# Norm statistics and residual moved from VectorE to ScalarE and TensorE in a recurrent block with routed experts

## The reference

```python
x = layernorm(x + attn(x))          # over the 256 channels, no gain
x = layernorm(x + experts(x))
```

```python
kv  = k_t[i] * v_t[j]
y_t = sum_i r_t[i] * (S[i, j] + u[i] * kv)
S   = w_t[i] * S + kv
```

## Time and profile before

| | |
|---|---|
| median of three runs | 2342.44 us |
| the profiled execution, its own time | 2343.03 us |
| its span, first to last instruction | 2341.3 us |
| mean granted TensorE clock | 0.922 of 2.4 GHz |
| PE (TensorE matmul) busy | 1938.1 us (83%) |
| DVE (VectorE) busy | 1834.2 us (78%) |
| POOL (GpSimd) busy | 1373.3 us (59%) |
| ACT (ScalarE) busy | 1059.1 us (45%) |
| 1400 to 2280 us, the experts: PE busy | 875.23 us |
| 2280 to 2342 us, the last norm: ACT, DVE busy | 37.65 us, 32.24 us |

### The profile page before, as it was taken

How to read it: one execution, slowest core, us unless ns; L and a number is a source line. 1 busy time by engine, 2 the same in 40 slices (tenths; PEclk the granted TensorE clock), 3 DMA queues, 4 the chain that set the end, 5 groups by cost and what they waited for, 6 DMA issues and landing times. The chain is left out here.

```text
span 2341.3 us, 33041 instructions
## 1 busy us (share of the span) xinstructions
PE 1938.1 (83%) x9894; PEld 1336.8 (57%) x9894; DVE 1834.2 (78%) x3157; ACT 1059.1 (45%) x1919; POOL 1373.3 (59%) x954
## 2 busy tenths in 40 slices
PE   5777888788777887877776299999999999999980
PEld 2333343333333333433332189999999999999970
DVE  2899999899999998999997266666666666666655
ACT  2233553345334543444432255555555555555546
POOL 3667787768777787678775224444444444454440
PEclk9889999899989998999886599999999999999995
DMA  6932111111112111111020144545454545455538
GB/s 163 220 87 64 46 46 54 47 54 36 51 47 58 29 51 42 58 29 49 31 69 20 58 122 121 122 121 120 120 120 122 120 120 121 120 123 122 124 57 287
DMA packets 172844, 209.00 MB, mean 89 GB/s; under 512 B 12796, under 2 KB 152480, under 8 KB 172768
## 3 DMA queue, kind: packets, MB, share of 16 engines
q1 hardware_dynamic: 112688, 143.09, 20.7%
q0 software_dynamic: 28672, 34.78, 8.6%
q10 hardware_dynamic: 31408, 30.33, 5.0%
HBM read 118.65 MB, written 75.53 MB: 83 GB/s over the span
## 5 line engine op out<-in xcount | busy, mean ns | idle before, releaser
L807 DVE TENSOR_TENSOR_SCAN S<-wT,S,vb 128x512 f32<-128x512 f32 x512 | 624.9, 1262 | 0.0
L1070 POOL TENSOR_TENSOR prod<-S,rT 128x2048 f32<-128x2048 f32 x128 | 536.8, 4198 | 148.0 <-DVE S L807 147.8
L1289 PE MATMUL up<-x_parts,w_parts 128*128 128x308 f32 x3072 | 464.2, 307 | 1.5 <-DVE x_parts L1402 1.5
L1304 PE MATMUL down<-w_parts,h_parts 128*128 128x512 f32 (+1 forms) x1280 | 452.4, 396 | 0.0
L1289 PEld LDWEIGHTS up<-x_parts,w_parts 128*128 128x128 f32 x3072 | 439.2, 189 | 4.1 <-issue 1.8
L1364 POOL TENSOR_TENSOR ye<-ye,weight 128x256 f32<-128x256 f32 (+1 forms) x160 | 197.7, 1235 | 379.9 <-DVE ye L1458 379.9
L1342 ACT ACTIVATE h_full<-up,b_now 128x616 f32<-128x616 f32 x256 | 198.6, 776 | 421.2 <-PE up L1289 409.6
L1372 POOL DMA_INDIRECT sums<-ye,sum_at x160 | 281.6, 1760 | 150.1 <-POOL ye L1364 140.0
L1445 DVE TENSOR_TENSOR h_parts<-h_full,h_parts 128x616 fp32r<-128x616 f32 x256 | 206.8, 808 | 193.1 <-ACT h_parts L1342 192.8
L1307 PE MATMUL down<-w_parts,h_parts 128*128 128x256 f32 (+1 forms) x1280 | 357.4, 279 | 0.0
L571 PE MATMUL vb<-v_stack,pick_v 128*128 128x512 f32 x512 | 216.7, 507 | 152.0 <-DVE S L807 151.8
(11 more groups left out here) (176 smaller groups left out, 2645.2 us busy)
## 6 DMA issues: line engine op xcount, KB each, us to landing
w_raw<-in_L_ffn_w_dram SPq DMA_DIRECT2D x64, 1024.0 KB, 8.8
expert_in_rows<-y_tok ACTq DMA_DIRECT2D x30, 652.5 KB, 9.1
xe<-expert_in_rows SPq DMA_DIRECT2D x32, 522.0 KB
v_stack<-v_parts SPq DMA_DIRECT2D x64, 256.0 KB, 4.5
x_tok<-in_L_attn_x_dram SPq DMA_DIRECT2D x16, 512.0 KB, 3.3
x_res<-in_L_attn_x_dram SPq DMA_DIRECT2D x16, 512.0 KB, 3.4
sums<-x_row SPq DMA_DIRECT2D x16, 512.0 KB, 2.9
rows<-sums SPq DMA_DIRECT2D x16, 512.0 KB, 5.5
```

The lines of the kernel that those rows point to most:

```text
L807: dve.tensor_tensor_scan(line[:, 1:TC + 1], wT[:, par, half, :], vb[:, p % 2, g, :], line[:, 0:1], ALU.mult, ALU.add).then_inc(scanned, 1)
L1070: pool.tensor_tensor(prod[:, q % 2], S[:, q % RING, :, 0:TC], rT[:, par, half, None, :].to_broadcast([P, QUAD, TC]), ALU.mult).then_inc(pr ...
L1289: last = pe.matmul(up[:, f % 2, half, 0:HC], w1_parts[:, par, wp, k, f * P:(f + 1) * P], x_parts[:, par, xp, k, half * HC:(half + 1) * HC] ...
L1304: pe.matmul(down[0:m, (par * TILES + t) % 2, :, :], h_parts[:, 0, f, t * P:t * P + m], w2_parts[:, par, :, f, :], start=f == 0, stop=False)
```

## The change

`stat1` and `stat2` leave VectorE. ScalarE drains y tile by tile with a sum along the 256 columns (`accum_out`), scales the sums to the negated mean, and takes the squares of the rows less the mean, again with a sum; the root then takes the sum of squares with a scale of 1/256. The residual leaves VectorE too: TensorE adds x_res by a matmul with the identity into the same accumulation as the projection, and ScalarE drains the result into x1, with sums. In `C_AT` the steps from "stat1" to "root2" come one slot sooner; "norm2", "x1T", "gate", "top" and "ratio" come one slot later; "count", "place" and "scatter" stay. In the last norm a partition holds four successive rows instead of rows that lie 128 apart.

```diff
@@ -186,8 +186,9 @@
         y_tok = sb("y_tok", [P, TPC, C])
         x_res = sb("x_res", [P, TPC, C])
         x1_row = sb("x1_row", [P, TPC, C + FIELDS])
-        stats = sb("stats", [P, 2, TPC, 6])
-        mv = sb("mv", [P, 2, TPC, 2])
+        total = sb("total", [P, 2, TPC])
+        square = sb("square", [P, 2, TPC])
+        squares = sb("squares", [P, TPC, C])
         rstd = sb("rstd", [P, 2, TPC])
         offset = sb("offset", [P, 2, TPC])
         minus_mean = sb("minus_mean", [P, 2, TPC])
@@ -259,6 +260,7 @@
         res_loaded = sem("res_loaded")
         x1_stored = sem("x1_stored")
         s_dve = sem("s_dve")
+        squared = sem("squared")
         root_done = sem("root_done")
         normed = sem("normed")
         tanh_done = sem("tanh_done")
@@ -320,13 +322,13 @@
         NSHORT = len(DVE_MIXES) * NH
         XM_OF = {"w": 0, "k": 1, "v": 2, "r": 0}
 
-        C_AT = {"turn": 6, "stat1": 9, "root1": 10, "norm1": 12, "back": 14, "wo0": 17, "z0": 18, "wo1": 19,
-                "z1": 20, "stat2": 21, "root2": 22, "norm2": 23, "x1T": 25, "gate": 27, "top": 28, "ratio": 28,
+        C_AT = {"turn": 6, "stat1": 8, "root1": 9, "norm1": 11, "back": 13, "wo0": 16, "z0": 17, "wo1": 18,
+                "z1": 19, "stat2": 20, "root2": 21, "norm2": 24, "x1T": 26, "gate": 28, "top": 29, "ratio": 29,
                 "count": 30, "place": 30, "scatter": 31}
         NCF = 10
 
-        LN1_AT = 2 * TPC + 1
-        X1_AT = LN1_AT + 2 * TPC + 1
+        LN1_AT = 1
+        X1_AT = LN1_AT + 1
         GAP_AT = X1_AT + 2 * TPC + 1
         HITS_AT = GAP_AT + 4
         NCH = HITS_AT + 2
@@ -527,11 +529,15 @@
                         last.then_inc(c_full, 1)
                     if s == C_AT[f"wo{k}"]:
                         c_fill(i, 4 + k)
+                        if k == 0:
+                            pe.wait_ge(res_loaded, stage_value(i, 16, 16))
                         for t in range(2):
+                            pe.matmul(pc[:, t * C:(t + 1) * C], ident[:], x_res[:, 2 * k + t, :],
+                                      start=True, stop=False)
                             for h in range(NH):
                                 at = (2 * k + t) * P
                                 last = pe.matmul(pc[:, t * C:(t + 1) * C], yT[:, h, at:at + P],
-                                                 wo_sb[:, h, :], start=h == 0, stop=h == NH - 1)
+                                                 wo_sb[:, h, :], start=False, stop=h == NH - 1)
                         last.then_inc(c_full, 1)
                     if s == C_AT["x1T"] + k:
                         c_fill(i, 6 + k)
@@ -716,37 +722,9 @@
                 dve.wait_ge(root_done, stage_value(i, 2, which + 1))
                 dve.reciprocal(rstd[:, which, :], rstd[:, which, :]).then_inc(s_dve, 1)
 
-            def statistics(src, which):
-                for t in range(TPC):
-                    dve.bn_stats(stats[:, which, t, :], src[:, t, :]).then_inc(s_dve, 1)
-
             def stage_c(i, par, s):
-                if s == C_AT["stat1"]:
-                    dve.wait_ge(c_drained, stage_value(i, NCF, 2))
-                    statistics(y_tok, 0)
-                    chain(i, TPC)
-                    dve.sem_inc(wait_carrier, 1)
-                    for t in range(TPC):
-                        dve.bn_aggr(mv[:, 0, t, :], stats[:, 0, t, :]).then_inc(s_dve, 1)
                 if s == C_AT["norm1"]:
                     invert(i, 0)
-                for k in range(2):
-                    if s == C_AT[f"z{k}"]:
-                        dve.wait_ge(c_full, stage_value(i, NCF, 5 + k))
-                        if k == 0:
-                            dve.wait_ge(res_loaded, stage_value(i, 16, 16))
-
-                            wait_from(dve, x1_stored, stage_value(i, 16, 0))
-                            wait_from(dve, scattered, stage_value(i, 16 * 2 * TPC, 0))
-                        dve.tensor_tensor(x1[:, 2 * k:2 * k + 2, :], pc[:].rearrange("p (t c) -> p t c", t=2),
-                                          x_res[:, 2 * k:2 * k + 2, :], ALU.add).then_inc(c_drained, 1)
-                if s == C_AT["stat2"]:
-                    dve.wait_ge(c_drained, stage_value(i, NCF, 6))
-                    statistics(x1, 1)
-                    chain(i, LN1_AT + TPC)
-                    dve.sem_inc(wait_carrier, 1)
-                    for t in range(TPC):
-                        dve.bn_aggr(mv[:, 1, t, :], stats[:, 1, t, :]).then_inc(s_dve, 1)
                 if s == C_AT["norm2"]:
                     invert(i, 1)
                 if s == C_AT["top"]:
@@ -907,8 +885,19 @@
                         if isinstance(i, int) and i == 0:
 
                             act.wait_ge(s_fill, 16 * FILLS)
-                        act.activation(y_tok[:, 2 * k:2 * k + 2, :], pc[:].rearrange("p (t c) -> p t c", t=2),
-                                       ACT.Copy).then_inc(c_drained, 1)
+                        for t in range(2):
+                            ins = act.activation(y_tok[:, 2 * k + t, :], pc[:, t * C:(t + 1) * C], ACT.Copy,
+                                                 accum_out=total[:, 0, 2 * k + t:2 * k + t + 1])
+                        ins.then_inc(c_drained, 1)
+                    if s == C_AT[f"z{k}"]:
+                        act.wait_ge(c_full, stage_value(i, NCF, 5 + k))
+                        if k == 0:
+                            wait_from(act, x1_stored, stage_value(i, 16, 0))
+                            wait_from(act, scattered, stage_value(i, 16 * 2 * TPC, 0))
+                        for t in range(2):
+                            ins = act.activation(x1[:, 2 * k + t, :], pc[:, t * C:(t + 1) * C], ACT.Copy,
+                                                 accum_out=total[:, 1, 2 * k + t:2 * k + t + 1])
+                        ins.then_inc(c_drained, 1)
                     if s == C_AT["back"] + k:
                         act.wait_ge(c_full, stage_value(i, NCF, 3 + k))
                         for h in range(NH):
@@ -919,13 +908,22 @@
                         act.wait_ge(c_full, stage_value(i, NCF, 7 + k))
                         act.activation(yT[:, :, 2 * k * P:(2 * k + 2) * P], pc[:].rearrange("p (h t) -> p h t", h=NH),
                                        ACT.Copy).then_inc(c_drained, 1)
+                for which, (name, rows) in enumerate((("stat1", y_tok), ("stat2", x1))):
+                    if s == C_AT[name]:
+                        act.wait_ge(c_drained, stage_value(i, NCF, 2 + 4 * which))
+                        act.activation(minus_mean[:, which, :], total[:, which, :], ACT.Copy, scale=-1.0 / C
+                                       ).then_inc(mean_kept, 1)
+                        act.wait_ge(mean_kept, stage_value(i, 2, which + 1))
+                        for t in range(TPC):
+                            ins = act.activation(squares[:, t, :], rows[:, t, :], ACT.Square,
+                                                 bias=minus_mean[:, which, t:t + 1],
+                                                 accum_out=square[:, which, t:t + 1])
+                        ins.then_inc(squared, 1)
                 for which, name in enumerate(("root1", "root2")):
                     if s == C_AT[name]:
-                        act.wait_ge(s_dve, stage_value(i, NCH, (2 * TPC, LN1_AT + 2 * TPC)[which]))
-                        act.activation(rstd[:, which, :], mv[:, which, :, 1], ACT.Sqrt, bias=eps_col[:, 0:1]
-                                       ).then_inc(root_done, 1)
-                        act.activation(minus_mean[:, which, :], mv[:, which, :, 0], ACT.Copy, scale=-1.0
-                                       ).then_inc(mean_kept, 1)
+                        act.wait_ge(squared, stage_value(i, 2, which + 1))
+                        act.activation(rstd[:, which, :], square[:, which, :], ACT.Sqrt, bias=eps_col[:, 0:1],
+                                       scale=1.0 / C).then_inc(root_done, 1)
                 for which, (name, rows, ready) in enumerate((("norm1", y_tok, LN1_AT), ("norm2", x1, X1_AT))):
                     if s == C_AT[name]:
                         act.wait_ge(s_dve, stage_value(i, NCH, ready))
@@ -1505,7 +1503,7 @@
         normed = sem("normed")
 
         def rows_of(dram, first, g):
-            return dram[bass.ds(g * (GT * P) + first, GT * P), :].rearrange("(t p) c -> p t c", p=P)
+            return dram[bass.ds(g * (GT * P) + first, GT * P), :].rearrange("(p t) c -> p t c", t=GT)
 
         def groups(eng, body):
 
```

## The result

The changed kernel takes **2385.36 us** (median of four runs, 2379.91 to 2386.41) where the kernel before, beside it on the same chip, takes 2341.84: a ratio of **1.0183, interval 1.0165 to 1.02**. Its profiled execution has a span of 2384.4 us, 43.1 more than before.

The account below looks back on a forecast made before the run. Two chains, VectorE's and that through GpSimd's mixes, TensorE and the gate, meet at the logits. From 2343.0 us: +41 for 14 bodies, -2 last body, +8 tail, -1 last norm = 2389; own range 2358 to 2430.

Parts of the forecast that it names:

- What bounds the kernel: Each body: VectorE's chain and the GpSimd mixes, K, gate chain arrive together at the logits; only shortening both shortens a body.
- The central step: Late in each body: later norm, 6.2 us to the gate, logits 3.7 us later, VectorE stalls some 4 us.
- ScalarE's terms: ScalarE in each body: accumulator 0.15 us, 0.6 per tile of residual or y, 0.67 per square, norm ending at 733.95.
- ScalarE without a gap: Sign to look for: ScalarE has no idle time from the second z to the norm.
- The tail: Chunk 15's stage C, standing alone: some 8 us longer, of which 3.6 from last y drain to first root.
- The clock: TensorE's wait for the norm halves its clock, costing 2.4 us, counted in half the bodies: 1.2 us a body.
- The sum: Whole kernel: 2343.0 + 41 - 2 + 8 - 1 = 2389 us, with 79.9 us a body against 77.0 on average.
- VectorE's gain: VectorE alone would gain 5.3 to 6.1 us a body; nothing of it survives the late gate.
- The residual on TensorE: Identity matmuls at the projection: 0.8 us for each half, the second half hidden under R0's wait.
- The first (VectorE stays the bound, 2296 us): Rival: VectorE bounds the bodies, 3.8 us less each, 2296 us in all; chance 0.22.
- The second: Rival: on ScalarE Square needs its own table load and Exp another, 2.6 us more a body, 2425 us; chance 0.05.
- The third: Rival: parts cancel, accumulators nearly free, clock holds, mixes come sooner; within 5 us of 2343; chance 0.06.

Follow-up runs that it names:

- first norm alone: Kernel before with only the first norm's statistics moved to ScalarE (sums in y drains, squares); slots, residual, second norm untouched: 2333.26 us, ratio 0.9971.
- half of the scatter: Changed kernel with each token's second expert left out of the scatter in the bodies: 2365.4 us, ratio 1.011 to the kernel before.
- The first experiment: Changed kernel with logits and choice of experts in slot 30 instead of 29, count and place in 31: 2335.18 us, ratio 0.9982 to the kernel before.
- the undone late step: Changed kernel with norm2, x1T, gate, top and ratio back in their old slots, earlier steps still one slot sooner: 2344.31 us, ratio 1.0025 to before.
- the layout alone: Kernel before with only the last norm's new token layout, four neighbouring tokens on a partition: 2340.59 us, ratio 0.9995.
- the slots' 63 us alone: Kernel before with only norm2, x1T, gate, top and ratio one slot later, no work moved: 2404.08 us, ratio 1.0279.
- inverse apart: Changed kernel, norm, transposes, gate in old slots, VectorE's second inverse alone in slot 24; logits in 28 or 29: 2344.17 or 2339.19 us.
- root early: Changed kernel with the second root in slot 19 ahead of the decays, norm, transposes and gate two slots sooner, logits one: 2356.79 us, ratio 1.007 to before.

## Why the prediction was right, and where it was right by luck

**What bounds the kernel: right.** Two chains that meet at the logits. The change takes 73 us of work from VectorE and the time rises (changed kernel); 25 us taken from it alone give back 8 (first norm alone); shortening only GpSimd's chain gives 1.2 us a body (half of the scatter).

**The central step: right.** The norm behind R1's drain, then 6.2 us to the gate: 6.3. The logits were to come 3.7 us later than before on the axis of pair 15 (71.6 against 67.9); they come at 758.32 - 687.63 = 70.7, 2.8 later. A wait of some 4 us a body, 3 to 5 by its signs: 4.56 to 4.60 in five of the fourteen bodies, 6.1 to 6.4 in nine. The first experiment and the undone late step show that this wait is the loss.

**ScalarE's terms: too large.** A square was put at 0.67 and is started every 0.49 us (740.99, 741.50), a tile of y or residual at 0.6 and starts every 0.37 (1324.98, 1325.35 below). The accumulator is a separate record of 0.19 us, and the next ACTIVATE starts 0.09 us into it (741.41, 741.50). Four squares are 2.0 us and not 2.7. For the same reason "ScalarE without a gap" was wrong: it waits 0.48 and 0.74 us for R0 and R1, and R1 on TensorE sets the norm's start as much as ScalarE does. The norm ends 64.3 us after pair 15, forecast 65.3. The tail, +5.5 instead of +8, is off by the same term: from the last y drain to the first root it took 1329.47 - 1324.98 = 4.5 us, where the forecast had 2.6 + 3.6 = 6.2.

```profile
1324.98 0.38 ACT L889 ACTIVATE y_tok<-pc 128x256 f32<-128x256 f32 x1 [0.74 <-PE pc L519]
...
1325.35 0.38 ACT L889 ACTIVATE y_tok<-pc 128x256 f32<-128x256 f32 x1
...
1328.18 1.28 ACT L925 ACT_TABLE_LOAD   x1
1329.47 0.30 ACT L925 ACTIVATE rstd<-square,eps_col 128x4 f32<-128x4 f32 x1
```

**The clock: right in kind, in more bodies.** The granted clock fell behind the wait for the norm in nine bodies instead of seven, and these are the nine in which the logits wait 6.1 to 6.4 us, 1.6 longer than in the five that kept 1.00. Body 12, TensorE in stretches of 2 us:

```profile
1069.00:1071.00 2.00, 0.51 (x2) 0.07 (x1) 2.00 (x4) 1.97 (x6) 2.00 (x2) 1.00 0.00 0
1071.00:1073.00 2.00, 1.53 (x7) 0.91 (x8) 2.00 (x2) 0.92 (x2) 2.00 (x1) 0.92 0.27 94
1073.00:1075.00 2.00, 2.00 (x8) 1.74 (x7) 0.04 (x1) 1.00 (x4) 0.97 (x1) 0.50 0.50 173
1075.00:1077.00 2.00, 2.00 (x10) 0.16 (x8) 0.00 (x0) 1.16 (x1) 0.00 (x0) 0.72 0.00 0
```

After the wait for the norm the granted clock falls to 0.50, the 1.2 GHz level, while transposes and products run.

**The sum: right by two errors that cancel.** The prediction worked out one body, 75.0 to 78.7 us, added 1.2 for the clock, and then held 79.9 against the average body of 77.0. The body it had worked out was one of the shorter ones: the thirteen intervals between logits of the kernel before run from 74.66 to 79.12 us. Like against like, its terms give 78.7 - 75.0 + 1.2 = +4.9 us a body, +69 in all, 2417 us. The same body measured went from 75.01 to 77.78, +2.8, and the average body from 76.98 to 79.82, +2.8. What the text lost by the mixed comparison (2.0) it had put on too much in ScalarE's terms (0.9 at the logits) and in its comparison of clocks: the nine longer waits are worth 9 x 1.6 / 14 = 1.0 a body, but the average body before lay 2.0 above its worked one too, and what of that was clock was never set against the 1.2. Consistently reckoned it would still have said slower, and been 32 us too high.

**VectorE's gain: right in kind.** "Nothing that VectorE gained survives" holds, with one cover not foreseen: besides the logits, VectorE waits 42 us for spreads from TensorE (10 before), most of them in pieces of 1.0 to 1.6. Pair 14 ended 66.1 us after pair 15 of the body before (753.75 - 687.63) and not 67.4.

**The residual on TensorE** was put at 0.8 a half, "the second half is hidden": alone on the kernel before it costs 1.2 us a body.

**Small terms.** Last body -1.7 (forecast -2). Last norm -0.8 (forecast -1); the layout alone can't be told from nothing.

**Rivals.** The first (VectorE stays the bound, 2296 us) was to decide at a norm's end of 63.6 us on the axis of pair 15 (732.3 - 668.65). It was 64.3, only 0.7 behind, but its 2296 was far away all the same: with the wait gone the time was 2335.18, since the spreads came late. The second is refuted: 128 squares on ScalarE have no ACT_TABLE_LOAD of their own, and the root's stay at 30. The table-set list in the Trainium skill, "ScalarE: Activation LUTs", section "Table sets: the hidden batching unit", doesn't name Square; here it ran between Exp and Sqrt without a load. The load is 1.28 us in the row (744.32), and the root starts 1.29 us after it. That page's section "What ACT_TABLE_LOAD costs" has the load at about 1.28 us too, and comes to 2.66 us for a switch with a drain of about 1.38 us, which no row here shows. The third (the parts cancel, within 5 us of 2343) had the accumulators right, nearly free, but the clock did not hold in nine bodies, and where it held the logits still waited 4.6 us.

**What stays open.** How much of the slots' 63 us alone goes through the gate's own lateness and how much through the next body's K was not separated. The late spreads for the pairs have two releasers in the traces, the drain of the y sums behind the norm (inverse apart) and the table load ahead of the decays (root early); the many pieces of about 1 us in the changed kernel stay unexplained (the identity matmuls, R and the own-value products are ahead of them in TensorE's order, but no run took one of those away).

## What to carry to other kernels

Work moved off the busiest engine pays only as far as the other chain into the same meeting point has slack: move the part whose place on the other engine has room (here the first norm, -0.29%), and be wary of the part that lies on the other chain. Here the residual alone cost 0.86%; the second norm's statistics were never moved alone, and with everything moved and the logits one slot later the kernel still came to -0.18%. In a loop scheduled by slots a step put later costs whatever stands behind it in every in-order queue; look for the first instruction that waits, and move the waiting one before giving the change up: here one slot for the logits was worth 50 us. And hold a body that was worked out against the same body, never against an average.

## What was not expected of the hardware

An accumulating ACTIVATE is followed by a record of its own, ACTIVATION_READ_ACCUMULATOR, of 0.19 us, yet only 0.09 us of it lies ahead of the next ACTIVATE: 256 columns from SBUF start every 0.49 us with bias and sum, while the plain norm of 256 columns with scale and bias does four in 2.07 (0.52 each).

The same wait did not always have the same effect on TensorE's clock. Cut at the start of the transposes, bodies 8 and 12 look alike: TensorE busy 2.00 of 2 us (748.09 to 750.09; 1067.47 to 1069.47), then 0.04 of 2 us with a wait of 1.96 for the norm, then 2.00 again. In body 8 the granted clock stayed at 1.00 throughout; in body 12 it was 0.81 in the last of these stretches and 0.50 in the next (1073.47 to 1075.47). All fourteen bodies have this wait (1.96 to 1.97 us) with the same busy times ahead of it; five kept the clock and nine did not. What decides between them these rows do not show.

A VectorE instruction can be long without doing more work: `gap`, four columns, took 0.15 us where no GpSimd product ran beside it, and up to 2.27 us where one did (the first experiment), ending each time with the product.
